# Weight maxima taken chunk by chunk, and the block transpose evicted by ScalarE

## The chip, the cores and the metric

The kernel runs on all 8 cores of one Trainium2 chip. Each core takes one of the eight sequences of the batch (8192 tokens of 1024 channels) through the whole layer, and the cores exchange nothing. The metric is the device time of the slowest core, in microseconds (us). Engines are called as the profile calls them: PE (TensorE, with PEld for its weight loads), DVE (VectorE), ACT (ScalarE), POOL (GpSimd) and SP (SyncE). POOL and SP only issue transfers here.

## The reference

One post-norm layer: linear attention with a causal mask inside, a LayerNorm, an FFN with 8-bit fake-quantized weights and a low-rank addition, and a second LayerNorm.

```python
q, k, v = x @ Wq.T, x @ Wk.T, x @ Wv.T            # 8 heads of 128
o   = causal_linear_attention(q, k, v)            # running state k^T v
z   = cumsum(k); o = o / max(|sum(q*z)|, 1)
x1  = layernorm(x + rmsnorm(o) @ Wo.T)
# FFN; fake_quant: scale = max|W| / 127 over the whole matrix
h   = gelu(x1 @ (fq(Wfc) + 2*Bfc@Afc).T + b)
y   = layernorm(x1 + h @ (fq(Wproj) + 2*Bproj@Aproj).T + b)
```

The scale of the fake quantization needs the largest magnitude of a whole weight matrix before any of its weights can be quantized. Both FFN matrices hold 4096 x 1024 values.

## The kernel before

The program is written out by hand: the Python code appends each instruction to its engine's list, in the order in which the code runs, and adds semaphore waits. Each engine executes its list strictly in order. `P.op` also makes an instruction wait for all earlier operations on its own semaphore, so two operations of one engine do not overlap, and a DMA issued by SP waits until SP's DMA before it has landed.

**First pass** (`for t in range(NT1)`, 16 tiles of 512 tokens). A tile has two parts.

- *Projections*: 24 groups of 8 matmuls (`qkv_groups`, L275 and L298), each into one of three PSUM banks in turn (pR0, pR1, pD) and evicted to SBUF alternately by ACT (L287, L310) and DVE (L284, L307). A group can start once the group three places ahead of it has been evicted. From the fifth group on, one step of the *tail* of the tile before is emitted after each group: squares on ACT (L322), their sums on DVE (L325), a chain of small operations, then, for each block of 128 tokens, scaling on DVE (L360), transposes on PE (L376, L383) with ACT evictions (L388, L391), the output projection (L401) and the residual sums on DVE (L408, L412).
- *Chunks*: 4 chunks of 128 tokens (`for ic in range(CPT)`). In each, PE transposes k (L556) and makes scores (L565), ACT evicts the transposes (L572, L574), DVE masks the scores (L577, L579) and copies the running state to bf16 (L584), PE makes the state update (L595, L601), DVE adds it to the state (L606, L610, L614), PE makes the output (L627 to L647) and ACT evicts it (L655 to L659). After each chunk one *late step* of the tile before is emitted: in chunk 0 the LayerNorm statistics `s_ln` (small DVE operations L442 to L459 around an ACT square root), in the others the normalized output on ACT (L469) and its store.

**Weight maxima.** `emit_wmax_job` loads 512 KB of an FFN matrix into the only staging tile `wst_sb` (SP DMA, L247), reduces its magnitudes on DVE (L249) and folds them into the running maximum (L252). The next load waits for that fold, since the tile is shared. There are 64 such jobs, 4 per tile of the first pass, and before the change all 4 are emitted in a row behind the four chunks. The scales made from the maxima are needed only at the end of the pass.

**Second pass** (`for t in range(NT2)`, 32 tiles of 256 tokens). Tile 0 also quantizes the weights (64 jobs, L770 to L814, on ACT and DVE above all). In each tile, PE transposes x1 by 16 matmuls against the identity into four PSUM banks (L894), the four banks are evicted into `x1_fm` (L902), and then 32 times: 8 matmuls into pA or pB (L920), Gelu on ACT (L927), and 4 matmuls into the four pH banks (L938), one step behind. Four bias matmuls (L978) close the tile, and DVE adds the four pH banks to x1 (L989). The first L920 group of a tile waits for all four evictions (L902) and for all four sums (L989) of the tile before. The second LayerNorm of a tile (`emit_ln2`, L826 to L864) is emitted in the next tile, ahead of the fifth L920 group.

Of the kernel before, what the change touches and what calls it, by code (L numbers as in the profile page):

```python
# [93 lines left out]
def build_program(S=8192, debug=False):  # L94
# [32 lines left out]
    P = Prog()  # L127
# [56 lines left out]
    with contextlib.ExitStack() as s1:  # L184
# [58 lines left out]
        def emit_wmax_job(job):  # L243
            wsrc, inner, acc = job
            P.wait("sync", fr["wst"])
            t_ws = P.op("sync", "ld", lambda e, s=wsrc:
                        e.dma_start(out=wst_sb[:], in_=s), 16)  # L247
            P.wait("vector", t_ws)
            P.op("vector", "ve", lambda e: e.reduce_max(  # L249
                wtmp[:], wst_sb[:], axis=AXX, apply_absolute_value=True))  # L250
            fr["wst"] = P.op("vector", "ve",
                             lambda e, a=acc: e.tensor_max(a[:], a[:], wtmp[:]))  # L252

        wmax_jobs = []
# [262 lines left out]
        for t in range(NT1):  # L517
# [30 lines left out]
            for ic in range(CPT):  # L548
# [115 lines left out]
                fr["pD"] = dn_toks[ic]  # L664
                if late_steps:
                    late_steps.pop(0)()
            while late_steps:
                late_steps.pop(0)()

            for jj in range(4 * t, 4 * t + 4):  # L670
                if jj < len(wmax_jobs):
                    emit_wmax_job(wmax_jobs[jj])

            fr["ostg"] = None
            tail_steps, late_steps = make_tail(t, xb, oev_toks, dn_toks, msq_gate)
# [17 lines left out]
    with contextlib.ExitStack() as s2:  # L693
# [12 lines left out]
        x1_fm = sb2("x1_fm", [128, 2 * D], BF16)  # L706
# [161 lines left out]
        for t in range(NT2):  # L868
# [18 lines left out]
            banks4 = [pA, pB, pU1, pU2]  # L887
# [7 lines left out]
                                  x1f16[:, i_ * D + d_ * 128:i_ * D + d_ * 128 + 128],  # L895
                                  ident16[:], start=True, stop=True))
            tk = P.close("tensor", "pe")
            P.wait("vector", tk)
            ev_t = {}
            for r in range(4):  # L900
                ev_t[r] = P.op("vector", "ve", lambda e, pq_=banks4[r], r_=r:
                               e.tensor_copy(x1_fm[:, r_ * 512:r_ * 512 + 512], pq_[:]))  # L902
            fr2["x1f16"] = ("pe", P.counts["pe"])
            fr2["pA"], fr2["pB"] = ev_t[0], ev_t[1]
            fr2["pU1"], fr2["pU2"] = ev_t[2], ev_t[3]
# [175 lines left out]
```

How the kernel before makes its waits and increments, by code:

```python
        def f(e, _b=build_fn, _s=sem, _n=n):  # L46
            ins = _b(e)
            ins.then_inc(self.sems[_s], _n)
            return ins
# [22 lines left out]
        def f(e, _s=sem, _v=v):  # L72
            e.wait_ge(self.sems[_s], _v)
```

## Time and profile before

| | us |
|---|---|
| two timed runs | 4656.39 and 4957.86 (median 4807.13) |
| the profiled execution, its own time | 4660.48 |
| its span, slowest core (core 3) | 4658.9 |
| spans of the eight cores | 4634.4 to 4658.9 |

PE is busy for 74% of the span, ACT for 33%, DVE for 31%. The mean granted TensorE clock is 0.85 of full speed on every core. The sum in the prediction is made against the profiled execution, 4660.48 us, which lies beside the lower of the two timed runs. Rows of the profile give times from the start of the span; a bracket behind a row is the idle time of the engine before it and what ended it.

### The profile page before, as it was taken

What the parts mean: (1) busy time and instruction counts of PE and PEld (TensorE: products, weight loads), DVE (VectorE), ACT (ScalarE), POOL (GpSimd) and SP (SyncE); (2) the same over time, 40 slices, a digit from 0 to 9 for tenths busy, and PEclk for the clock granted to TensorE, in tenths of its full rate; (3) what the DMA queues carried; (4) which work ended last, traced back from release to release, by engine and by line L of the source; (5) the groups of instructions that cost most, each with busy time, mean ns of one, the idle gap of its engine ahead of it and who ended that gap; (6) DMA issues with size and microseconds to landing.
All of it is one profiled execution on the core that took longest, in us unless ns stands there. A gap on an engine that the chain in (4) does not pass through costs nothing.

```text
span 4658.9 us, 61505 instructions; the slowest of 8 cores (4634.4 to 4658.9 us)
## 1 busy us (share of the span) xinstructions
PE 3433.0 (74%) x21768; PEld 2044.8 (44%) x21768; DVE 1428.6 (31%) x2098; ACT 1516.0 (33%) x2513; POOL 131.9 (3%) x217
## 2 busy tenths in 40 slices
PE   0777666777777777633368889888888898888887
PEld 0433333333333333311135556555555565555554
DVE  0333333333333334348851111211211112112111
ACT  0233333333232333348862322223223222232232
POOL 0000000000000000000000000000000000000000
PEclk9888888888888888765579989899899898898998
DMA  6122222222222222123310000100100001001000
GB/s 108 46 64 64 64 64 64 64 64 64 64 59 63 57 54 68 50 73 105 104 64 25 31 31 25 37 28 28 37 25 31 31 25 37 28 28 37 24 32 19
DMA packets 77970, 231.28 MB, mean 50 GB/s; under 512 B 7760, under 2 KB 24400, under 8 KB 77664
## 3 DMA queue, kind: packets, MB, share of 16 engines
q1 hardware_dynamic: 36368, 134.80, 8.9%
q0 software_dynamic: 41312, 92.55, 7.5%
q8 instruction: 189, 3.10, 0.3%
q14 instruction: 101, 0.83, 0.1%
HBM read 185.65 MB, written 67.11 MB: 54 GB/s over the span
## 4 chain that ended last, share of the span: by engine, by line
PE 59%; DVE 15%; ACT 12%; DMA 7%; issue 6%; DVEq 1%; ACTq 0%; SPq 0%; POOL 0%; POOLq 0%
PE pH L938 19%; PE pA L920 10%; PE pB L920 9%; PE pOA L401 4%; PE pR L275 3%; PE pOB L401 3%; PE pR L298 2%; DMA wst_sb<-wfcT 2%; DMA wst_sb<-wprojT 2%; DVE r L989 2%; DVE x_fm L902 2%; PE pD L298 2%; DVE osq L360 2%; DVE wtmp L249 2%; ACT out L834 2%
## 5 line engine op out<-in xcount | busy, mean ns | idle before, releaser
L938 PE MATMUL pH<-WpjT,h 128*128 128x512 bf16 x4096 | 1116.6, 398 | 117.7 <-ACT h L927 117.7
L920 PE MATMUL pA<-x_fm,WfcT 128*128 128x256 bf16 x4096 | 600.5, 295 | 174.4 <-DVE x_fm L902 174.4
L938 PEld LDWEIGHTS pH<-WpjT,h 128*128 128x128 bf16 x4096 | 412.5, 102 | 435.7 <-issue 183.1
L920 PEld LDWEIGHTS pA<-x_fm,WfcT 128*128 128x128 bf16 x4096 | 429.6, 106 | 375.1 <-issue 215.2
L920 PE MATMUL pB<-x_fm,WfcT 128*128 128x256 bf16 x4096 | 566.4, 284 | 0.0
L927 ACT ACTIVATE h<-pA,bfc_sb 128x256 bf16<-128x256 f32 x512 | 242.8, 474 | 971.5 <-PE pA L920 970.3
L989 DVE TENSOR_TENSOR r<-pH,x1tm 128x512 f32<-128x512 f32 x128 | 88.6, 692 | 1365.2 <-PE pH L978 1354.9
L920 PEld LDWEIGHTS pB<-x_fm,WfcT 128*128 128x128 bf16 x4096 | 416.0, 102 | 173.8 <-issue 13.3
L927 ACT ACTIVATE h<-pB,bfc_sb 128x256 bf16<-128x256 f32 x512 | 242.9, 474 | 613.7 <-PE pB L920 609.9
L275 PE MATMUL pR<-x_fm,WqT 128*128 128x512 bf16 x768 | 216.9, 442 | 301.9 <-DVE q_sb L284 191.7
L275 PEld LDWEIGHTS pR<-x_fm,WqT 128*128 128x128 bf16 x768 | 81.5, 109 | 418.4 <-issue 354.9
L401 PE MATMUL pOA<-WoT,o2f_sb 128*128 128x512 bf16 x512 | 171.3, 495 | 76.3 <-ACT o2f_sb L391 76.3
L595 PE MATMUL pR<-v_sb,ktm_sb 128*128 128x128 bf16 x512 | 58.0, 283 | 195.4 <-DVE state_sb L584 103.8
L408 DVE SCALAR_TENSOR_TENSOR r<-pOA,x_tm 128x512 f32<-128x512 f32 x64 | 44.2, 691 | 437.4 <-PE pOB L401 437.4
L275 PE MATMUL pR<-x_fm,WkT 128*128 128x512 bf16 x640 | 148.4, 379 | 0.0
L249 DVE TENSOR_REDUCE wtmp<-wst_sb 128x1 f32<-128x1024 f32 x64 | 78.1, 1220 | 223.8 <-DMA wst_sb<-wfcT 114.0
L298 PE MATMUL pR<-WvT,x_fm 128*128 128x512 bf16 x640 | 146.0, 379 | 0.0
L595 PEld LDWEIGHTS pR<-v_sb,ktm_sb 128*128 128x128 bf16 x512 | 44.1, 126 | 206.1 <-issue 206.1
L401 PE MATMUL pOB<-WoT,o2f_sb 128*128 128x512 bf16 x512 | 130.9, 401 | 0.0
L655 ACT CAST o_stg<-pOA 128x512 bf16<-128x512 f32 x64 | 37.5, 586 | 276.7 <-PE pD L647 276.7
L401 PEld LDWEIGHTS pOA<-WoT,o2f_sb 128*128 128x128 bf16 x512 | 55.6, 117 | 159.0 <-issue 135.9
L287 ACT CAST q_sb<-pR 128x512 bf16<-128x512 f32 x48 | 28.1, 586 | 289.6 <-PE pR L275 288.1
(166 smaller groups left out, 3881.2 us busy)
## 6 DMA issues: line engine op xcount, KB each, us to landing
x_tm<-x SPq DMA_DIRECT2D x16, 2048.0 KB, 8.1
x1s<-x1o POOLq DMA_DIRECT2D x64, 512.0 KB, 3.3
x1tm<-x1s SPq DMA_DIRECT2D x32, 1024.0 KB, 4.8
y<-out POOLq DMA_DIRECT2D x64, 512.0 KB, 3.2
wst_sb<-wfcT SPq DMA_DIRECT2D x32, 512.0 KB, 4.1
x_fm<-xT POOLq DMA_DIRECT2D x16, 1024.0 KB, 10.1
wst_sb<-wprojT SPq DMA_DIRECT2D x32, 512.0 KB, 4.0
wstg<-wfcT SPq DMA_DIRECT2D x32, 512.0 KB, 4.1
```

What stands on the lines that cost most here:

```text
L249: P.op("vector", "ve", lambda e: e.reduce_max(wtmp[:], wst_sb[:], axis=AXX, apply_absolute_value=True))
L275: e.matmul(pq[:], W[:, d_ * D + h_ * HD:d_ * D + h_ * HD + HD], x_fm[:, d_ * T1:(d_ + 1) * T1], start=(d_ == 0), stop=(d_ == 7)))
L298: e.matmul(pq[:], x_fm[:, d_ * T1 + i_ * 128:d_ * T1 + i_ * 128 + 128], WvT[:, d_ * D + hf * 512:d_ * D + hf * 512 + 512], start=(d_ == 0) ...
L360: ap = P.op("vector", "ve", lambda e: e.tensor_tensor(osq_sb[j % 2][:].rearrange("p (c f) -> p c f", f=128), o_stage[:, j * D:(j + 1) * D] ...
L401: e.matmul(p[:], o2f_sb[:, h_ * 128:h_ * 128 + 128], WoT[:, h_ * D + hf * 512:h_ * D + hf * 512 + 512], start=(h_ == 0), stop=(h_ == 7)))
L595: e.matmul(p[:, (h_ % 4) * 128:(h_ % 4) * 128 + 128], ktm_sb[:, h_ * 128:h_ * 128 + 128], v_sb[:, i_ * D + h_ * 128:i_ * D + h_ * 128 + 12 ...
L834: sqs.append(P.op("scalar", "ac", lambda e, ii=i2, bb=b: e.activation(out_sb[0][:], r2_sb[bb][:, ii * D:(ii + 1) * D], AF.Square, accum_ou ...
L902: e.tensor_copy(x1_fm[:, r_ * 512:r_ * 512 + 512], pq_[:]))
L920: e.matmul(p[:, 0:T2], WfcT[:, d_ * FF + f_ * 128:d_ * FF + f_ * 128 + 128], x1_fm[:, d_ * T2:(d_ + 1) * T2], start=(d_ == 0), stop=(d_ == ...
L927: gel[hb] = P.op("scalar", "ac", lambda e, f_=fc, bb=hb: e.activation(h1_sb[bb][:], (pA if bb == 0 else pB)[:, 0:T2], AF.Gelu, bias=bfc_sb ...
L938: e.matmul(pH[ii * 2 + hf][:], h1_sb[bb][:, ii * 128:ii * 128 + 128], WpjT[:, f_ * D + hf * 512:f_ * D + hf * 512 + 512], start=(f_ == 0), ...
L989: e.tensor_add(r2_sb[bb][:, ii * D + hf * 512:ii * D + hf * 512 + 512], pH[ii * 2 + hf][:], x1_tm[bb][:, ii * D + hf * 512:ii * D + hf * 5 ...
```

## The change

Two edits. The four weight-maximum jobs of a first-pass tile are emitted one behind each chunk (after that chunk's late step) in place of all four behind the last one. The four evictions of the second pass's block transpose (L902) go from DVE's `tensor_copy` to ACT's `copy`.

```diff
                 if late_steps:
                     late_steps.pop(0)()
+                jj = 4 * t + ic
+                if jj < len(wmax_jobs):
+                    emit_wmax_job(wmax_jobs[jj])
             while late_steps:
                 late_steps.pop(0)()
-
-            for jj in range(4 * t, 4 * t + 4):
-                if jj < len(wmax_jobs):
-                    emit_wmax_job(wmax_jobs[jj])
@@
             tk = P.close("tensor", "pe")
-            P.wait("vector", tk)
+            P.wait("scalar", tk)
             ev_t = {}
             for r in range(4):
-                ev_t[r] = P.op("vector", "ve", lambda e, pq_=banks4[r], r_=r:
-                               e.tensor_copy(x1_fm[:, r_ * 512:r_ * 512 + 512], pq_[:]))
+                ev_t[r] = P.op("scalar", "ac", lambda e, pq_=banks4[r], r_=r:
+                               e.copy(x1_fm[:, r_ * 512:r_ * 512 + 512], pq_[:]))
```

## Rows read from the trace of the kernel before

**Rows 1.** The page's first line.

```profile
span 4658.9 us, 61505 instructions; the slowest of 8 cores (4634.4 to 4658.9 us)
```

**Rows 2.** Windows, one per pass: PE, PEld, DVE, ACT, POOL busy; PEclk; DMA.

```profile
192.00:2057.00 1865.00, 1282.66 (x8247) 698.09 (x8248) 706.63 (x1217) 562.64 (x910) 51.38 (x80) 0.81 0.21 62
2413.00:4659.00 2246.00, 1932.49 (x12524) 1249.04 (x12522) 401.65 (x570) 634.35 (x1215) 42.74 (x64) 0.90 0.08 30
```

**Rows 3.** Waits of the whole run: who for whom, us, times, longest us.

```profile
PE pR L275 <- DVE q_sb L284: 191.7, 15, 13.8
...
PE pA L920 <- DVE x_fm L902: 174.4, 31, 5.9
...
DVE wtmp L249 <- DMA wst_sb<-wfcT: 114.0, 24, 6.0
```

**Rows 4.** Timeline between two first-pass tiles, DVE and then PE: start, us, instruction.

```profile
1251.13 1.22 DVE L249 TENSOR_REDUCE wtmp<-wst_sb 128x1 f32<-128x1024 f32 x1
...
1252.46 0.16 DVE L252 TENSOR_TENSOR wmax_pj<-wmax_pj,wtmp 128x1 f32<-128x1 f32 x1
...
1271.19 1.49 DVE L284 CAST q_sb<-pR 128x512 bf16<-128x512 f32 x2
...
1257.67 1.89 PE L275 MATMUL pR<-x_fm,WqT 128*128 128x512 bf16 x8
...
1272.03 3.57 PE L275 MATMUL pR<-x_fm,WqT 128*128 128x512 bf16 x8 [12.46 <-DVE q_sb L284]
```

**Rows 5.** Windows of 10 us behind that stall, first and last of 15.

```profile
200.15:210.15 10.00, 10.00 (x34) 3.89 (x35) 3.79 (x4) 4.25 (x5) 0.00 (x0) 0.71 0.70 254
...
1862.84:1872.84 10.00, 10.00 (x34) 3.93 (x35) 3.78 (x4) 4.35 (x6) 0.00 (x0) 0.73 0.61 236
```

**Rows 6.** Timeline of chunks 1 and 2 of a first-pass tile.

```profile
1229.73 0.69 DVE L577 TENSOR_TENSOR sTm_sb<-pSA,mask_s 128x512 bf16<-128x512 f32 x1
...
1232.16 1.01 PE L595 MATMUL pR<-v_sb,ktm_sb 128*128 128x128 bf16 x8 [3.40 <-DVE state_sb L584]
...
1237.31 0.69 DVE L577 TENSOR_TENSOR sTm_sb<-pSA,mask_s 128x512 bf16<-128x512 f32 x1 [2.02 <-PE pSB L565]
...
1240.09 0.90 PE L595 MATMUL pR<-v_sb,ktm_sb 128*128 128x128 bf16 x8 [2.95 <-ACT ktm_sb L574]
```

**Rows 7.** Line L577: DVE's idle time before it, us and times.

```profile
  PE pSB L565: 63.8, 48
```

**Rows 8.** Timeline behind the last first-pass tile, ACT and DVE.

```profile
1965.86 2.20 ACT L322 ACTIVATE osq<-o_stg 128x1024 bf16<-128x1024 bf16 x2
...
1980.86 5.19 DVE L325 TENSOR_REDUCE rowsA<-osq 128x8 f32<-128x1024 bf16 x4
```

**Rows 9.** Timeline between two second-pass tiles.

```profile
3631.21 3.08 DVE L989 TENSOR_TENSOR r<-pH,x1tm 128x512 f32<-128x512 f32 x4 [43.22 <-PE pH L978]
...
3631.43 0.61 PE L894 MATMUL pU<-ident,x1f 128*128 128x128 bf16 x8
...
3634.40 0.69 DVE L902 CAST x_fm<-pA 128x512 bf16<-128x512 f32 x1
...
3637.62 1.87 PE L920 MATMUL pA<-x_fm,WfcT 128*128 128x256 bf16 x8 [5.58 <-DVE x_fm L902]
```

**Rows 10.** Windows behind that stall, behind the LayerNorm stall, and after.

```profile
3637.60:3643.20 5.60, 5.58 (x23) 3.40 (x24) 2.59 (x3) 0.95 (x2) 0.00 (x0) 0.50 0.18 71
...
3652.88:3656.88 4.00, 4.00 (x15) 2.10 (x16) 0.07 (x1) 0.90 (x2) 0.53 (x1) 0.57 0.35 135
3656.90:3700.00 43.10, 43.10 (x300) 29.24 (x299) 2.73 (x3) 11.39 (x24) 0.83 (x1) 1.00 0.03 13
```

**Rows 11.** Groups of ACT while the weights are quantized: count, busy us, mean ns.

```profile
L781 ACT CAST lora_sb<-pU 128x512 bf16<-128x512 f32 x64 | 37.5, 586 | 27.5 <-PE pU L773 19.9 <-DVE WfcT L814 2.2 <-DVE WpjT L814 1.6
...
L927 ACT ACT_TABLE_LOAD x1 | 1.3, 1283 | 0.1
```

## The prediction

> **What bounds the kernel now.** I read the windows by pass first. They show a first pass of some 1865 us and a second pass, once the weights are quantized, of 2246 us [rows 2]; the span is 4658.9 us [rows 1]. PE is the engine that sets the end in both: in the second pass it is busy for 1932.49 of 2246 us, with DVE at 402 and ACT at 634. In the first pass it is busy for only 1283 of 1865 us, so something makes it wait. The mean granted clock is 0.81 and 0.90 of full speed, a mixture of its two levels, 2.4 and 1.2 GHz.
>
> Next I read the waits. Two of PE's concern this change: 191.7 us in 15 waits for a DVE eviction of q (L284), and 174.4 us in 31 waits for the evictions L902 [rows 3]. The same view says what holds DVE up in the first case: its reduction L249 waits for the load of the weights, 114.0 us in 24 waits for Wfc, and 107.8 us in as many for Wproj.
>
> The timeline between two tiles shows how the first wait arises [rows 4]. DVE starts the first weight job at 1251.13 and gets to the q evictions only at 1271.19, 20 us later: four jobs of about 1.5 us each, and three loads between them which cannot start before the job ahead is done. PE has meanwhile filled its three banks. The fourth group ends at 1259.56 (1257.67 + 1.89), and the fifth starts at 1272.03, after 12.46 us of idle time. When it starts, it is slow: 3.57 us for a group of 8 matmuls that took 1.89 before.
>
> **Edit 1: the jobs spread over the chunks.** The same 64 reductions, folds and loads are issued; only their place changes.
>
> *What goes.* Behind the last chunk there is one job, not four. It takes from 1251.13 to 1252.62, and the first DVE eviction it could delay is that of the second group, whose matmuls end about 1256. So the stall goes whole. 191.7 us / 15 = 12.78 us a tile, together 191.7 us.
>
> *What the clock gives back.* Behind the stall PE runs at 1.2 GHz for a while. In the 10 us windows behind the 15 restarts PE is busy throughout, and the granted clock is 0.71 in the first, 0.73 in the last, and 0.70 to 0.83 over all fifteen, 0.76 in the mean [rows 5]. So 10 us x 0.24 = 2.4 us of full-speed work is lost each time. Without the idle time nothing there lets the clock fall: in the groups ahead of the stall it had risen, 1.89 us a group. I count 2.4 x 15 = 36 us. Bounds: 0 (the tail's chain on ACT and DVE absorbs it; it ends in PE's next stall, 2.5 us) and 3.0 x 15 = 45 (the lowest of the windows).
>
> *The last tile.* No groups follow it. ACT has the first squares ready at 1965.86 + 1.06 = 1966.9, and DVE begins their sums only at 1980.86, behind the jobs [rows 8]. They would start at 1967.0: 13.9 us.
>
> *What it costs in the chunks.* A job occupies DVE from 1251.13 to 1252.62, and with one gap between operations (0.10 us) 1.59 us. Behind it in DVE's list stands the mask L577 of the next chunk, and behind that the state copy L584, for which PE's L595 may wait. Two kinds of chunk have to be told apart [rows 6]:
>
> - Into chunks 2 and 3, DVE is idle before L577: 2.02 us in the row, and over the run 63.8 us in 48 waits [rows 7]. 16 of these are the first chunks of tiles, at 0.20 us, 3 us in sum; the other 32 have 1.9 us each. A job of 1.59 us fits. PE's L595 waits there for ACT's eviction L574 anyway. Cost: 0.
> - Into chunk 1, L577 starts without idle time, right behind `s_ln`, and L595 waits 3.40 us for DVE's state copy. The job of chunk 0 comes between, and everything behind it shifts by 1.59 us. It happens in the 15 tiles that have a `s_ln`: 15 x 1.59 = 23.9 us.
> - Bounds: 0, and 1.59 for all 48 chunks that follow a job within a tile, 76 us.
>
> *Are the loads in time?* From fold to landing DVE waited 114.0 / 24 = 4.75 us, at most 6.0 us [rows 3]. The job of chunk 0 would end at about 1231.2; the next one's turn comes at 1237.31 - 2.02 + 1.59 = 1236.9, 5.7 us later. A mean load is 0.9 us early, the longest one 0.3 us late, which the 0.43 us left of the idle time takes. The later loads have a whole chunk of nearly 8 us. SP's load of x for the next tile now queues behind the fourth job's load, and is wanted tens of us later. Cost: 0; if every load of a chunk were 1 us late beyond its cover, 45 us.
>
> Edit 1: 191.7 + 36 + 13.9 - 23.9 = 217.7 us.
>
> **Edit 2: L902 from DVE to ACT.** The timeline between two tiles of the second pass [rows 9]: the transposes end at 3631.43 + 0.61 = 3632.04. DVE is then in the four sums L989 until 3634.29, and makes the four evictions from 3634.40 to 3637.48; PE goes on at 3637.62, after 5.58 us.
>
> On ACT nothing stands between: its last Gelu is long done, and the LayerNorm comes later in its list. The casts start at 3632.04 + 0.15 = 3632.2. A cast of this very form, 128x512 from f32 PSUM to bf16, takes 586 ns on ACT [rows 11], against 0.69 us on DVE [rows 9]. With a gap of 0.09, four take 4 x 0.586 + 3 x 0.09 = 2.6 us, so they end at 3634.8, and PE goes on at 3634.95. The sums L989 run beside them and end 0.5 us sooner, which is the cover that this leaves. Gain 3637.62 - 3634.95 = 2.67 us, x 31 = 82.7 us. The first tile has no sums in the way and gains four times 0.11 and a little, 0.5 us. DVE is relieved of 3.1 us, off the path.
>
> The Trainium skill ("ScalarE: Activation LUTs", Rules for kernel authors) sends elementwise work to VectorE, which it calls up to about three times faster than ScalarE in bf16. By it an ACT cast would take up to 2.1 us, the four 8.4 us, and the edit would lose some 3 us a tile, 100 us in all. The rows disagree: 586 ns on ACT against 0.69 us on DVE for this form.
>
> *The clock.* Behind this stall PE works 5.60 us at 0.50, which loses 2.8 us [rows 10]. Behind the shorter stall of 3.68 us in which PE waits for the LayerNorm's work on ACT, the window is 4.00 us at 0.57 and loses 1.7 us. The new stall is 2.9 us, but light work (16 short transposes, 4 matmuls on one partition) stands in front of it. I take 2.0 us lost, nearer to the shorter stall: 0.8 us gained, x 31 = 24.8 us. Bounds: 0 (as now), and 2.8 x 31 = 87 us (the clock does not fall).
>
> Edit 2: 82.7 + 0.5 + 24.8 = 108.0 us. A tile should go from 71.7 to 68.2 us.
>
> **Sum.** 217.7 + 108.0 = 325.7 us off the profiled execution's 4660.5: **4335 us**. The median shown, 4807, lies 147 us above that execution, between two runs 301 us apart; I forecast against the execution whose rows I read.
>
> **Rivals.**
>
> - *The clock gives nothing back.* The idle time goes, and PE meets a low clock elsewhere instead. For it: the level falls in every tile at several places. Against it: both stalls are followed by a slow stretch. Without 36 and 24.8 us: 4396 us.
> - *The chunks have no cover.* Each job delays its chunk by 1.59 us, or its load is late by that. For it: the cover is only 0.43 us over the job. Against it: 1.9 us of idle time in 32 chunks. 33 more x 1.59 = 52 us: 4387 us; with late loads (45) 4432.
> - *ACT's casts bring table loads.* One to the copy and one back to Gelu, 2 x 1.28 us x 31 = 80 us: 4415 us. Against it: 64 pairs of such casts stand among Gelus with one table load in all [rows 11]. This would be a change that does not do what it says.
> - *The clock does not fall at all between tiles* of the second pass. The loss of 2.8 goes whole: 62 us more, 4273 us. Against it: the light stretch of 2 us before the gap.
> - *Slower: the chip grants less than full speed once the cores work more densely.* PE spends roughly 2500 us busy at full speed (1932 and 1283 us busy, less a quarter at the low level). The gain of 326 us is used up where that level is granted at 1 / (1 + 326/2500) = 0.885. At 0.80 it would cost 2500 x 0.25 = 625 us: 4960 us. Against it: 43.1 us of PE without a gap ran at 1.00, with all eight cores at work [rows 10]. The Trainium skill ("TensorE: Matmul & The Clock Gate", Part 1) knows such a limit, 13/16 of the clock for a whole die once three of its cores run dense matmuls; no stretch of these rows shows it.
>
> **How the numbers follow.** Forecast 0.58; clock gives nothing 0.12; chunks without cover 0.10; table loads 0.04; no fall at all 0.12; slower by the clock 0.04. The range 4270 to 4425 takes in all but the last and the worst of the second. A measurement of this kernel tells about 2% (93 us) from no change. All cases but the last gain more than that; I leave 0.02 of them to a sum of several costs. Of the last, 0.03 ends slower and 0.01 within 2%. Faster 0.94, same 0.03, slower 0.03.
>
> **What would show it.** The wait of PE L275 for L284 falls from 191.7 us to nearly nothing; L249 waits for its DMA almost never. The start-to-start time of first-pass tiles falls by 12.78 + 2.4 - 1.59 = 13.6 us. L577 of chunk 1 starts 1.6 us later against L614, and chunks 2 and 3 keep their length. In the second pass PE waits 2.9 us, now for ACT, in place of 5.6, and the L902 casts last 586 ns with no table load beside them. I am wrong if L249 stands in the chunks waiting for its load, if a new wait of the same size appears in the projections, or if the dense windows show less than 1.00.

## The result, and the profile after

| | before | changed |
|---|---|---|
| profiled execution, us | 4660.48 | 4351.28 |
| its span, slowest core | 4658.9 | 4349.6 |
| lowest of the timed runs | 4656.37 | 4350.23 |
| median of all timed runs | 4756.63 (10) | 4563.39 (11) |

The ratio is 0.936, 95% interval [0.933, 0.938]: faster by 6.4%. In seven of the eleven timed runs of the changed kernel, as in five of the ten of the kernel before, the cores of one die or of both were granted less clock and took longer; the ratios and times here and below leave such runs out, the medians of this table do not.

So the mechanism forecast 4335 us, the execution of the same kind took 4351, and the median over all runs, 4563, lies above the range of 4270 to 4425.

The page's first line and the windows of the two passes, with the columns of [rows 2]:

```profile
span 4349.6 us, 61567 instructions; the slowest of 8 cores (4341.2 to 4349.6 us)
...
191.00:1852.00 1661.00, 1252.33 (x8232) 695.93 (x8230) 702.90 (x1211) 562.61 (x910) 51.82 (x80) 0.83 0.27 67
2209.00:4349.00 2140.00, 1907.41 (x12524) 1238.22 (x12523) 315.87 (x446) 707.11 (x1339) 42.74 (x64) 0.94 0.08 31
```

The first pass went from about 1865 to 1661 us, the second from 2246 to 2140. Most of it is time around PE's work. PE's busy time itself fell too, at nearly the same number of matmuls: by 30 us in the first pass (1282.66 to 1252.33) and by 25 us in the second (1932.49 to 1907.41). That is what the higher clock gave back; its mean rose from 0.81 to 0.83 and from 0.90 to 0.94.

The waits of the changed kernel that answer to [rows 3], and DVE's idle time before L249:

```profile
PE pA L919 <- ACT x_fm L901: 94.0, 31, 3.4
...
PE pR L595 <- DVE state_sb L584: 141.0, 36, 5.9
...
  DMA wst_sb<-wfcT: 2.1, 2
  DMA wst_sb<-wprojT: 1.0, 2
```

PE's wait for L284, 191.7 us before, is no longer among the waits listed. DVE's wait for the loads went from some 222 us to 3.1. PE's wait between second-pass tiles went from 174.4 us behind DVE to 94.0 us behind ACT. (From the second pass on, a line's number is one less in the changed kernel: L902 is L901.)

DVE's timeline in chunks 0 to 2 of a first-pass tile:

```profile
1213.92 0.16 DVE L451 SCALAR_TENSOR_TENSOR rows<-rows 128x4 f32<-128x4 f32 x1
1215.43 0.18 DVE L458 RECIPROCAL rows<-rows 128x4 f32<-128x4 f32 x1 [1.35 <-ACT rows L455]
1215.71 0.16 DVE L459 SCALAR_TENSOR_TENSOR rows<-rows 128x4 f32<-128x4 f32 x1
1215.99 1.22 DVE L249 TENSOR_REDUCE wtmp<-wst_sb 128x1 f32<-128x1024 f32 x1
1217.31 0.16 DVE L252 TENSOR_TENSOR wmax_pj<-wmax_pj,wtmp 128x1 f32<-128x1 f32 x1
1217.57 0.69 DVE L577 TENSOR_TENSOR sTm_sb<-pSA,mask_s 128x512 bf16<-128x512 f32 x1
...
1222.97 0.17 DVE L614 TENSOR_TENSOR state_f<-state_f,pZ 128x8 f32<-128x8 f32 x1
1223.25 1.22 DVE L249 TENSOR_REDUCE wtmp<-wst_sb 128x1 f32<-128x1024 f32 x1
1224.57 0.16 DVE L252 TENSOR_TENSOR wmax_pj<-wmax_pj,wtmp 128x1 f32<-128x1 f32 x1
1224.84 0.69 DVE L577 TENSOR_TENSOR sTm_sb<-pSA,mask_s 128x512 bf16<-128x512 f32 x1
```

The job of chunk 0 stands where the prediction put it, from 1215.99 to 1217.57: 1.58 us ahead of chunk 1's mask. The second job starts as soon as the state is added; its data is there. The mask behind it starts without idle time, where the prediction left 0.43 us; over the run DVE is idle for 0.1 us in the mean before chunk 2's mask and for 0.55 us before chunk 3's.

The boundary between two second-pass tiles, to be held against [rows 9]:

```profile
3301.18 3.08 DVE L988 TENSOR_TENSOR r<-pH,x1tm 128x512 f32<-128x512 f32 x4 [42.48 <-PE pH L977]
3301.40 0.61 PE L893 MATMUL pU<-ident,x1f 128*128 128x128 bf16 x8
3302.16 0.59 ACT L901 CAST x_fm<-pA 128x512 bf16<-128x512 f32 x1 [3.28 <-PE pU L893]
3302.83 0.59 ACT L901 CAST x_fm<-pB 128x512 bf16<-128x512 f32 x1
3303.50 1.26 ACT L901 CAST x_fm<-pU 128x512 bf16<-128x512 f32 x2
3304.37 2.29 DVE L825 TENSOR_REDUCE rows<-r 128x2 f32<-128x2048 f32 x1
3305.01 1.03 PE L919 MATMUL pA<-x_fm,WfcT 128*128 128x256 bf16 x8 [3.00 <-ACT x_fm L901]
```

The casts follow the transposes at once and run beside DVE's sums. PE goes on 3.00 us after the last transpose, where it took 5.58. And it goes on at full speed: the first group takes 1.03 us, where it took 1.87. The slow stretch begins one group later.

### The profile page after: what moved, and what is told of

Same layout as the page of the kernel before. It is cut to its first block, busy times and chain, and to the rows that moved or that the text cites. A ratio compares the mean times of both kernels' runs of the same rounds, so it can differ in the third digit from the quotient of the medians.

```text
span 4349.6 us, 61567 instructions; the slowest of 8 cores (4341.2 to 4349.6 us)
## 1 busy us (share of the span) xinstructions
PE 3380.5 (78%) x21768; PEld 2033.4 (47%) x21768; DVE 1340.0 (31%) x1970; ACT 1591.2 (37%) x2641; POOL 132.3 (3%) x217
## 4 chain that ended last, share of the span: by engine, by line
PE 66%; ACT 13%; DVE 11%; issue 6%; DMA 4%; ACTq 0%; DVEq 0%; SPq 0%; POOL 0%; POOLq 0%
PE pH L937 20%; PE pA L919 10%; PE pB L919 10%; PE pR L275 5%; PE pOA L401 4%; PE pOB L401 3%; PE pR L298 3%; PE pD L275 2%; PE pD L298 2%; DVE osq L360 2%; ACT x_fm L901 2%; ACT out L833 2%; DVE rowsA L325 1%; PE pR L595 1%; ACT wstg L798 1%
## 5 line engine op out<-in xcount | busy, mean ns | idle before, releaser
L919 PE MATMUL pA<-x_fm,WfcT 128*128 128x256 bf16 x4096 | 580.1, 289 | 94.0 <-ACT x_fm L901 94.0
L926 ACT ACTIVATE h<-pA,bfc_sb 128x256 bf16<-128x256 f32 x512 | 242.9, 474 | 692.8 <-PE pA L919 691.6
L926 ACT ACTIVATE h<-pB,bfc_sb 128x256 bf16<-128x256 f32 x512 | 242.9, 474 | 603.9 <-PE pB L919 600.1
L275 PE MATMUL pR<-x_fm,WqT 128*128 128x512 bf16 x768 | 188.9, 403 | 110.8 <-DMA x_fm<-xT 110.2
L595 PE MATMUL pR<-v_sb,ktm_sb 128*128 128x128 bf16 x512 | 60.6, 292 | 225.8 <-DVE state_sb L584 141.0
L595 PEld LDWEIGHTS pR<-v_sb,ktm_sb 128*128 128x128 bf16 x512 | 45.9, 130 | 236.4 <-issue 236.4
L310 ACT CAST v_sb<-pR 128x512 bf16<-128x512 f32 x48 | 28.1, 586 | 260.2 <-PE pR L298 260.2
L863 POOL DMA_DIRECT2D y<-out x64 | 42.7, 668 | 2131.1 <-DVE out L858 2123.5
## 6 DMA issues: line engine op xcount, KB each, us to landing
x_fm<-xT POOLq DMA_DIRECT2D x16, 1024.0 KB, 13.7
```

Source lines behind the costliest of these rows:

```text
L275: e.matmul(pq[:], W[:, d_ * D + h_ * HD:d_ * D + h_ * HD + HD], x_fm[:, d_ * T1:(d_ + 1) * T1], start=(d_ == 0), stop=(d_ == 7)))
L595: e.matmul(p[:, (h_ % 4) * 128:(h_ % 4) * 128 + 128], ktm_sb[:, h_ * 128:h_ * 128 + 128], v_sb[:, i_ * D + h_ * 128:i_ * D + h_ * 128 + 12 ...
L919: e.matmul(p[:, 0:T2], WfcT[:, d_ * FF + f_ * 128:d_ * FF + f_ * 128 + 128], x1_fm[:, d_ * T2:(d_ + 1) * T2], start=(d_ == 0), stop=(d_ == ...
L926: gel[hb] = P.op("scalar", "ac", lambda e, f_=fc, bb=hb: e.activation(h1_sb[bb][:], (pA if bb == 0 else pB)[:, 0:T2], AF.Gelu, bias=bfc_sb ...
```

## The experiments

**The two edits, each alone.** e1 has the jobs behind each chunk and L902 on DVE; e2 is the reverse.

```diff
 e1: + emit_wmax_job(wmax_jobs[4 * t + ic])      # inside the chunk loop
     - for jj in range(4 * t, 4 * t + 4): emit_wmax_job(wmax_jobs[jj])
 e2: - P.wait("vector", tk) ... e.tensor_copy(x1_fm[...], pq_[:])
     + P.wait("scalar", tk) ... e.copy(x1_fm[...], pq_[:])
```

> Edit 1 alone (jobs one behind each chunk, L902 stays on DVE). If the two edits are independent, the first pass shortens as it did in the changed kernel, by about 205 us, and the second stays at 71.7 us a tile: about 4452 us. Rival: the edits share a cause (the clock, or the heat of denser work), then the two alone don't add up to the 308 us of both.

> Edit 2 alone (L902 on ACT, jobs stay behind the fourth chunk). Independent edits: first pass as before, with PE's 191.7 us of waiting for L284; second pass 68.3 us a tile, 105 us less in all: about 4552 us. Rival as for edit 1 alone: the sum of both gains would differ from 308 us by more than 10 us.

e1 took 4457 us (three runs within 4455.7 to 4458.6; ratio 0.957 [0.955, 0.959]), e2 4550.0 (one run). Against 4657 for the kernel before on that chip these are 200 and 107 us, 307 in all; both edits together gave 306 (4656.4 to 4350.2). They are independent, and each is worth what its pass of the trace shows. In e2 the first-pass stall stands untouched while the second pass has the changed kernel's wait:

```profile
PE pR L275 <- DVE q_sb L284: 194.8, 15, 15.1
...
PE pA L920 <- ACT x_fm L902: 93.9, 31, 3.4
```

**What the first-pass stall comes from: the reductions or the loads.** e3 is the kernel before with four staging tiles. The loads go out ahead of the chunks, the reductions stay in a row behind the fourth.

```diff
-wst_sb = sb1("wst_sb", [128, 1024], F32)
+wst_sb = [sb1(f"wst_sb{i}", [128, 1024], F32) for i in range(4)]
+for jj in range(4 * t, 4 * t + 4): emit_wmax_load(jj)     # ahead of the chunks
 for jj in range(4 * t, 4 * t + 4): emit_wmax_job(jj)      # behind them, as before
```

> The kernel before with four staging tiles for the weight jobs: the four loads are issued ahead of the chunks, the four reductions stay in a row behind the fourth chunk. Theory A, the stall comes from the loads that wait for the one tile: DVE is held for 4 x 1.59 = 6.4 us, until about 1257.5 where PE needs it by 1259.6, so PE's wait for L284 goes whole and no chunk grows: 15 x 15.1 + 12 = 239 us less, about 4418 us. Theory B, it comes from the reductions' own work in front of the evictions: a wait of 5 us or more stays in each of 15 tiles, and the gain is under 150 us, over 4510 us.

It took 4418 to 4430 us (three runs); ratio 0.950 [0.948, 0.952]. PE's wait for the q eviction is down to 1.1 us in all, and L249 (L255 here) waited 0.5 us for a load in the whole run:

```profile
L255 DVE TENSOR_REDUCE wtmp<-wst_sb x64: 1219/1220/1222, 185.0 to 1742.2; 128x1 f32<-128x1024 f32 x64
its engine sat idle before it (us, times) until:
  DMA wst_sb<-wprojT: 0.5, 1
```

So the four reductions in a row, 6.3 us of DVE work in front of the evictions, cost PE nothing. The whole stall was the three loads that waited for the one tile. With four tiles edit 1 isn't needed, and this form gains some 30 us more than e1 (4418 to 4430 against 4456 to 4459).

**What the jobs cost in the chunks.** e6 joins e3's four tiles with the casts on ACT. e7 is the changed kernel with chunk 0's job a few instructions earlier, in the wait inside `s_ln`.

```diff
 e7, in s_ln, behind the square root's issue on ACT:
+emit_wmax_job(wmax_jobs[4 * (t + 1)])       # no longer behind chunk 0
 P.wait("vector", t_sq)
 P.op("vector", "ve", lambda e: e.reciprocal(...))
```

> Four staging tiles, reductions in a row behind the fourth chunk, casts L902 on ACT. If the two parts are independent: 4657 less 237 (four tiles alone) less 105 (casts): about 4315 us, 35 us below the changed kernel, because no chunk carries a reduction and none waits for a load. Rival: the chunks' cost is made up elsewhere in the changed kernel, then both are equal at 4350.

> The changed kernel with the job of chunk 0 moved by a few instructions: into s_ln, between its variance and its reciprocal, where DVE waits some 1.3 us for ACT's square root. Theory A, the chunks of the changed kernel are 1.5 us longer a tile because this job stands ahead of chunk 1's mask: most of it now lies in the wait, 15 x 1.3 = 20 us less than the changed kernel, about 4332 us. Theory B, the other three jobs or late loads cost it: no change, 4352 us.

e6 took 4321 to 4329 us (ratio 0.928 [0.927, 0.930]), e7 4324 to 4327 (0.928 [0.927, 0.930]): both some 25 us under the changed kernel's 4350 to 4354. The expectation for e6 was 4315, some 10 us too low; why was not followed up. The time of the four chunks, from the first k transpose to the next tile's first projection, in us over 14 tiles of the slowest core. A chunk counts from its first k transpose to the next chunk's:

| | four chunks | chunk 0, 1, 2, 3 | projections | first-pass tile | second-pass tile |
|---|---|---|---|---|---|
| before | 30.81 | 6.70, 8.45, 7.87, 7.79 | 87.98 | 118.79 | 71.66 |
| changed | 32.84 | 6.77, 10.16, 8.00, 7.92 | 72.95 | 105.79 | 68.26 |
| e6 (no job in a chunk) | 30.82 | 6.80, 8.51, 7.74, 7.77 | 73.07 | 103.89 | 68.26 |
| e7 (chunk 0's job in `s_ln`) | 31.34 | 6.80, 8.96, 7.76, 7.82 | 72.69 | 104.03 | 68.30 |

The jobs lengthen the chunks by 2.03 us, not 1.59. 1.71 of it is in chunk 1, behind chunk 0's job. Chunks 2 and 3, behind the jobs of chunks 1 and 2, grew by 0.13 us each. e7 has these two jobs in the same places, and its chunks 2 and 3 are as short as e6's without them (7.76 and 7.82 against 7.74 and 7.77). So these two jobs cost next to nothing, as forecast. What e7 still has over e6, 0.5 us, is in chunk 1: the job takes 1.6 us in a wait of 1.35 us (L458 in the timeline above), so moving it takes back 1.2 of its 1.7 us.

**How near the loads are to being late.** e8 issues every load twice.

```diff
+for _twice in range(2):
     t_ws = P.op("sync", "ld", lambda e, s=wsrc: e.dma_start(out=wst_sb[:], in_=s), 16)
```

> The changed kernel with every load of a weight job issued twice in a row (SP waits for the first to land), so about 9 us from fold to landing in place of 4.6. The next job's turn in a chunk comes 5.7 to 8 us after the fold. Theory A, the loads are only just hidden: DVE waits some 3 us in each of two chunks a tile, 6 x 16 = 95 us more, about 4445 us, and L249 shows this wait. Theory B, loads had ample room: under 20 us more.

It took 4431.9 us (one run), 80 more than the changed kernel, near theory A's 95. DVE's wait for the loads came back inside the chunks, 97.2 + 72.3 = 169.5 us in 48 waits, and PE's wait for the state copy grew from 141 to 309 us (L249 and L595 are lines 250 and 596 here):

```profile
PE pR L596 <- DVE state_sb L585: 308.6, 63, 7.4
...
DVE wtmp L250 <- DMA wst_sb<-wfcT: 97.2, 24, 7.3
DVE wtmp L250 <- DMA wst_sb<-wprojT: 72.3, 24, 4.9
```

The loads are hidden in the changed kernel (3.1 us of waiting), but with little room: two in a row, some 9 us, no longer fit in a chunk.

**Does the clock follow the stall?** e4 makes each cast L902 twice, which brings the stall back to its old length with the change in place.

```diff
 for r in range(4):
+    for _twice in range(2):
         ev_t[r] = P.op("scalar", "ac", ... e.copy(x1_fm[...], pq_[:]))
```

> The changed kernel with each of the four casts L902 made twice by ACT. The stall between second-pass tiles grows by 4 x 0.675 = 2.7 us, to the 5.6 us of the kernel before. Theory A, the length of the stall sets also how long the clock stays at 1.2 GHz behind it: the tile goes back to 71.7 us, 31 x 3.4 = 105 us more, about 4455 us. Theory B, the stall costs its own length and no more: 31 x 2.7 = 84 us more, about 4434 us.

It took 4458.5 us (one run), some 106 more than the changed kernel's 4350 to 4354: theory A's 105, not B's 84. On core 2 of the profiled execution, which never showed less than the usual two levels, PE's wait for the casts was 173.2 us against 94.0, 79 more, and the second-pass tiles are 71.7 us apart again. The remaining 27 us are put down to the clock: PE's other wait in a tile is 3.7 us in both.

**Shortening the stall further.** e5 is e6 with a signal for each of the four PSUM banks. e9 also lets each pair of matmuls of the first group wait for its own cast alone, and moves the wait for DVE's sums to where the pH banks are first written.

```diff
 e5:      tks.append(P.close("tensor", "pe"))     # behind each bank's 4 transposes
          P.wait("scalar", tks[r])                # before cast r, not for all 16
 e9: -    P.wait("tensor", t_xfm); P.wait("tensor", fr2["pH"])
     +    if fc == 0 and dc % 2 == 0: P.wait("tensor", ev_all[dc // 2])   # in emit_h1
     +    if fc == 0: P.wait("tensor", fr2["pH"])                         # in emit_h2
```

> Four staging tiles with the reductions in a row behind the fourth chunk, the casts L902 on ACT, and each of the four PSUM banks signalled by itself, so that the first cast starts behind 4 transposes, not 16. Against the same kernel without the last part (e6): ACT starts 0.7 us sooner, then DVE's four sums L989 end last, 0.5 us before the casts did. 31 x 0.5 = 16 us less than e6, about 4300 us, if stalls cost their length; 0 if the clock takes it back.

> Four staging tiles, casts on ACT with one signal a bank, and in the first L920 group of a tile each pair of matmuls waits only for its own cast; the wait for DVE's sums L989 moves to the first use of the pH banks. The stall of 1.9 us between tiles (58.5 us in all in e5) is broken up: PE works through it at the pace of the casts. Theory A, without a gap the clock mostly stays at 2.4 GHz between tiles: tiles go from 67.9 us to the 65.4 us that single tiles of e5 show, 31 x 2.5 = 78 us less, about 4236 us. Theory B, the thin work there still lets the clock fall and only the gap's length is won: under 31 x 1.2 = 37 us, 4277 us or more.

e5 took 4314.2 us, ratio 0.927 [0.925, 0.930]. PE now waits for DVE's sums, as expected, and 58.5 us in place of 94.0. Of these 35.5 us only about 10 reached the end (67.94 us a tile, from 68.26): the clock took the rest back.

e9 took 4212 to 4229 us (three runs), ratio 0.904 [0.902, 0.906]. On the profiled core, core 1, tiles are 65.8 us apart in the mean. That mean holds three tiles of 68 to 75 us in a stretch of 150 us in which cores 0 and 1 were granted 0.81; without it, on cores 2 to 7, tiles are 64.9 to 65.0 us apart. The boundary, and ahead of it the wait that e5 had left:

```profile
PE pA L929 <- DVE r L998: 58.5, 30, 2.3
```

```profile
2490.23 0.59 ACT L911 CAST x_fm<-pA 128x512 bf16<-128x512 f32 x1 [2.64 <-PE pA L903]
2490.29 0.89 PE L903 MATMUL pU<-ident,x1f 128*128 128x128 bf16 x8
...
2491.09 0.38 PE L929 MATMUL pA<-x_fm,WfcT 128*128 128x256 bf16 x2
2491.63 0.38 PE L929 MATMUL pA<-x_fm,WfcT 128*128 128x256 bf16 x2 [0.17 <-ACT x_fm L911]
2492.30 0.38 PE L929 MATMUL pA<-x_fm,WfcT 128*128 128x256 bf16 x2 [0.29 <-ACT x_fm L911]
2492.98 0.39 PE L929 MATMUL pA<-x_fm,WfcT 128*128 128x256 bf16 x2 [0.29 <-ACT x_fm L911]
2493.21 1.03 PE L929 MATMUL pB<-x_fm,WfcT 128*128 128x256 bf16 x8
2494.25 1.02 PE L949 MATMUL pH<-WpjT,h 128*128 128x512 bf16 x4
```

The first fence is e5's wait, the second e9's timeline. In e9 the gap of 1.9 us is broken into three of 0.2 to 0.3 us, and the groups behind it run at 1.03 us: PE stays at 2.4 GHz. PE's wait for the casts is 23.2 us in all, 1.1 us a tile less than in e5, and the tile lost 2.9 us (67.9 to 65.0). Theory A holds. PE's busy time says where the rest is: 62.3 us a tile in e5, 60.5 on core 3 of e9. e9 is the best version found: it leaves the jobs where the kernel before had them, keeps edit 2, and is about 3% faster than the changed kernel (4212 to 4229 against 4350 to 4354).

**The range: which cores are granted less clock.** c1 is the changed kernel again, beside others on one chip.

> The changed kernel, unaltered, beside the others on one chip. In executions in which all eight cores are granted the full clock: 4350 to 4357 us, 0.935 of the kernel before. Theory A, its two edits have nothing to do with how often a die is granted less: over all kernels of this study, about half of the executions show it, with the edits and without. Theory B, denser work brings it on: more often here than in the kernel before, run beside it.

Four of its five runs took 4353 to 4368 us, ratio 0.935 [0.933, 0.937], and one 4649. The profile of e4 fell into an execution in which cores 4 to 7 were granted less, and cores 0 to 3 were not:

```profile
core 2: 4454.6 us, clock 0.855
...
core 5: 4668.1 us, clock 0.799
core 6: 4564.9 us, clock 0.814
```

Two stretches of it, first on core 5 and then on core 6 of the same die, with the columns of [rows 2]. PE is busy throughout in the first row of each:

```profile
3205.00:3235.00 30.00, 30.00 (x172) 18.51 (x171) 0.00 (x0) 7.01 (x15) 0.00 (x0) 0.81 0.00 1
230.00:250.00 20.00, 17.60 (x98) 8.44 (x96) 5.32 (x10) 8.70 (x15) 0.87 (x1) 1.00 0.00 1
```

```profile
3205.00:3235.00 30.00, 30.00 (x207) 20.13 (x206) 1.25 (x2) 8.37 (x18) 0.83 (x1) 1.00 0.05 19
230.00:250.00 20.00, 17.15 (x76) 7.25 (x74) 5.38 (x10) 4.66 (x8) 0.00 (x0) 0.81 0.00 1
```

In the same 30 us core 5 made 172 matmuls and core 6 207. Tiles on core 5 were 81.9 us apart there, against 71.7. Core 4 goes with core 5 and core 7 with core 6: the first pair has the level from 2938 us on, in the second pass, the second pair from 111 to 1934 us, in the first pass and the start of the second. It comes in small portions too, in executions that are hardly longer: 146 us on cores 0 and 1 in the profiled execution of c1 (4368 us), 152 us on the same two in that of e9.

The level of 0.81 is the one that the Trainium skill ("TensorE: Matmul & The Clock Gate", Part 1) gives for a die whose cores run dense matmuls, 13/16. The Trainium skill has the whole die enter it soon after a third core starts dense work and stay there while the load lasts; these runs show it on two cores of a die and not on the other two, and they show executions without it and others with it, of one and the same program.

Does the change bring it on? In the study's runs of the kernel before, 18 of 39 lie above 4700 us. Of the kernels with the casts on ACT (the changed kernel, e2, e4 to e9), 26 of 54 were so disturbed, and one of four each of e1 and e3. 46% and 48% are nearly equal, as theory A of c1 has it, but the counts are too uneven to rule out an effect of the change: five of six for e2 and e4 on one chip, none of six for e5 and one of six for e6 on another. What decides it in one execution stays open: nothing in these runs tells it.

## Why the prediction was right and wrong

**Wrong: the range.** The failing step is the last sentence of the sum, "I forecast against the execution whose rows I read", with the chance of 0.04 that the last rival got. It puts at nothing what the timed runs lose to the third level of the clock, 0.81. The times shown before had a median 147 us above that execution, from two runs 301 us apart. That was the sign that some executions take 6% longer, and it was set aside. Against the rival stood a window of 43.1 us at 1.00 [rows 10]; it shows one execution and says nothing of the others. The study's runs put the share of disturbed ones at about a half. In seven of the eleven timed runs of the changed kernel cores were granted less; these took 4541 to 4754 us, the other four 4350 to 4373. So the term put at nothing measured some 210 us in the median (4563). A range for the median of all runs should have reached to 1.065 times the forecast (4957.86 / 4656.39), about 4616 us, and stated the time without disturbance beside it. Which side of a half the eleven runs fell on was chance: with two fewer disturbed, the median would have lain inside the range, and the step would have been wrong all the same.

The rival's sign and size were wrong as well. It was called slower because the change would bring the lower clock on, at a cost of 625 us. The lower clock is there before and after, and the change remains faster with it: 4563 against 4757 in the medians. The longest of the eleven runs lies 403 us above the shortest.

**Right: the mechanism and the sum, to 5%.** Forecast 325.7 us, measured 309.2 in the profiled executions.

- *The stall goes whole* (191.7 us forecast). The wait is gone. With the clock, projections should have shortened by 12.78 + 2.4 = 15.2 us a tile; they did by 15.03 on the slowest core and by 14.0 to 14.9 on the others. Of the clock's 36 us, PE's busy time in the first pass shows some 30.
- *The reductions in front of the evictions cost nothing*: shown by e3.
- *Chunk 0's job costs its full 1.59 us*: chunk 1 grew by 1.71.
- *The jobs of chunks 1 and 2 cost nothing*: right to 0.13 us a chunk. DVE's idle time before L577 went from 63.8 us to 11.7, that is by 52 us, the length of 32 jobs. In 12 of the 14 tiles PE waited in chunk 2 for ACT's eviction and not for DVE, in chunk 3 in all. What makes up the 0.4 us a tile above 1.59 (0.12 in chunk 1, 0.33 in the three others) was not followed up.
- *The first tile* was taken as free; it grew by 0.95 us. *The last*, from its first projection to the second pass, shortened by 23.5 us, not by 15.2 + 13.9 - 1.6 = 27.5. Its stall did shrink as forecast, by 13.8 us; its projections gained 13.7 in place of 15.2, and the stretch from its first L376 to the second pass became 2.4 us longer, which was not followed up.
- *The loads are in time*: 3.1 us of waiting in all; e8 shows how little room there was.
- *The casts on ACT*: 586 ns, no table load beside them (32 + 31 loads of tables in the second pass, all at L847 and L926). The stall is 3.0 us, forecast 2.9, and 80.4 us went from the wait, against 82.7. The factor of three that the prediction sets against this is one for bf16, and these casts read f32 from PSUM: they are another case and do not contradict it.
- *The clock's 0.8 us a tile*: a tile went from 71.66 to 68.26, of which the wait is 2.6 and the clock 0.8. e4 shows it in reverse, 106 us for 79 us of added waiting, and PE's busy time in the second pass fell by 25 us, against 24.8 forecast. The second pass gave 105.3 us from tile 1 to the end, forecast 107.5.

In sum, the shortfall of 16.5 us is the chunks (6 for 14 tiles), the last tile (4), the second pass (2), the projections (2), and the first tiles of both passes (about 2).

## What to carry to other kernels

A stall behind an engine that "does four jobs" can be a stall behind one staging buffer: give the loads their own tiles and the jobs may stay where they are. A job laid into idle time of its engine is nearly free where the next engine waits for something else anyway (chunks 2 and 3), and costs its whole length where it does not (chunk 1); moving it by a few instructions into a wait of its own engine took most of that back. Where timed runs of one program differ by 6%, forecast the undisturbed time and the median of all runs separately; one traced execution shows only one of the two.

## What the runs showed of the hardware

- A gap in PE's work costs more than its length, and not in proportion. Between second-pass tiles 5.6, 3.0, 1.9 us of waiting gave tiles of 71.7, 68.3 and 67.9 us; only when the last gap was broken up did the tile fall to 65.0. From 5.6 to 3.0 us the clock added 0.8 us to the 2.6; from 3.0 to 1.9 it took back 0.8 of 1.1; from 1.9 us to scattered waits of 0.75 it added 1.8 to the 1.1. PE's busy time a tile goes the same way: 62.35, 61.55, 62.3 and 60.5 us.
- Behind the 3.0 us gap PE's first group still ran at 2.4 GHz (1.03 us), and the next ones at 1.2 (1.74 and 1.91 us) although PE was busy: here the clock fell after the gap, not in it. Behind the gap of 5.6 us already the first group was slow (1.87 us).
- A cast of 128x512 from f32 PSUM to bf16 took 586 ns on ACT and 692 on DVE, and a cast between Gelus brought no table load.
- The granted clock has a third level beside 1.0 and 0.5: 0.81. It came to cores in pairs (0 and 1, 4 and 5, 6 and 7), not to all four of a die at once, and for part of an execution: in one of e4 1431 us on core 5 and 1379 us on core 6, at different times, and none on cores 0 to 3.
